# Gate products of the second chunk moved behind the V blocks in a fused gated-delta-rule and spline-FFN kernel

## The reference

```python
q = short_conv(hidden_states @ Wq, conv_wq).reshape(b, t, NUM_HEADS, HEAD_K)
k = short_conv(hidden_states @ Wk, conv_wk).reshape(b, t, NUM_HEADS, HEAD_K)
v = short_conv(hidden_states @ Wv, conv_wv).reshape(b, t, NUM_HEADS, HEAD_V)
beta = jax.nn.sigmoid(hidden_states @ Wb)
g = -jnp.exp(A_log) * jax.nn.softplus(hidden_states @ Wa + dt_bias)
o = gated_delta_rule(q, k, v, g, beta)
gate = (hidden_states @ Wg).reshape(b, t, NUM_HEADS, HEAD_V)
o = o * jax.lax.rsqrt(jnp.mean(o * o, -1, keepdims=True) + EPS) * norm_weight
o = o * jax.nn.silu(gate)
return o.reshape(b, t, VALUE_DIM) @ Wo
```

## Time and profile before

| what | us |
|---|---|
| median of 3 runs | 807.68 |
| the three runs | 807.45, 812.63, 807.68 |
| the profiled execution | 812.1 |
| its span, first to last instruction | 810.3 |

### The profile page before, as it was taken

The page is one execution under the profiler, slowest core; times in us unless marked ns, Lnnn a source line. Parts: engine busy times, 40 slices in busy tenths (PEclk is TensorE's granted clock), DMA queues, the critical chain, the costliest instruction groups (busy, mean ns, idle before and its releaser), DMA issues.

```text
span 810.3 us, 15480 instructions
## 1 busy us (share of the span) xinstructions
PE 759.3 (94%) x5688; PEld 448.3 (55%) x5688; DVE 580.9 (72%) x1403; ACT 468.6 (58%) x1082; POOL 357.5 (44%) x393
## 2 busy tenths in 40 slices
PE   2979599999999999999899999999899999999998
PEld 1456267656657665656674656755344444444443
DVE  5789957878998979998978998577764544545320
ACT  3777835675795766796765687666643333333310
POOL 5148966675894653784663678123330000000000
PEclk9999958999999999999999999999999999999999
DMA  7420041140003022003022001168954414304111
GB/s 216 140 91 18 0 111 40 51 149 12 31 5 124 23 93 79 27 0 126 14 104 80 27 1 34 62 197 179 207 177 104 118 39 104 92 14 111 45 37 42
DMA packets 56113, 63.26 MB, mean 78 GB/s; under 512 B 18375, under 2 KB 41276, under 8 KB 56038
## 3 DMA queue, kind: packets, MB, share of 16 engines
q1 hardware_dynamic: 49430, 45.50, 20.0%
q0 software_dynamic: 4224, 13.11, 5.6%
q10 hardware_dynamic: 2384, 3.67, 1.3%
HBM read 33.69 MB, written 19.73 MB: 66 GB/s over the span
## 4 chain that ended last, share of the span: by engine, by line
PE 70%; DVE 20%; issue 4%; ACT 4%; POOL 1%; DMA 1%; DVEq 0%; POOLq 0%; ACTq 0%
PE bank L672 22%; PE pd L2121 7%; PE pd L2120 7%; PE pd L2119 7%; DVE bank L1213 3%; DVE inv L1219 3%; PE bank L768 2%; DVE cv L1115 2%; PE bank L916 2%; PE bank L861 2%; PE bank L839 2%; PE bank L892 2%; PE bank L759 2%; PE pu L2101 2%; PE pu L2102 2%
## 5 line engine op out<-in xcount | busy, mean ns | idle before, releaser
L672 PE MATMUL bank<-x_parts,w 128*128 128x512 f16 x576 | 137.0, 385 | 1.8 <-DVE x_parts L1072 1.5
L2188 DVE TENSOR_TENSOR hh<-sg,pu 128x512 f32<-128x512 f32 x64 | 43.9, 687 | 96.1 <-ACT sg L2158 91.2
L672 PEld LDWEIGHTS bank<-x_parts,w 128*128 128x128 f16 x576 | 59.4, 106 | 63.8 <-issue 6.8
L2066 POOL DMA_DIRECT2D yr<-y_attn x16 | 8.8, 552 | 181.8 <-DMA out<-yr 181.8
L672 PE MATMUL bank<-w,x_parts 128*128 128x384 f16 x384 | 80.9, 343 | 6.6 <-DVE inv L1219 6.6
L2158 ACT ACTIVATE sg<-pg 128x512 f32<-128x512 f32 x64 | 38.0, 595 | 71.0 <-PE pg L2102 71.0
L1115 DVE SCALAR_TENSOR_TENSOR cv<-raw,taps,cv 128x512 f32<-128x512 f32 x72 | 56.1, 829 | 0.6
L672 PEld LDWEIGHTS bank<-w,x_parts 128*128 128x128 f16 x384 | 37.0, 110 | 26.3 <-DVE inv L1219 7.4
L1739 POOL TENSOR_TENSOR rn<-t,mhalf 128x6 f32<-128x6 f32 x16 | 22.8, 1422 | 65.2 <-DVE t L1305 65.2
L1213 DVE TENSOR_TENSOR bank<-bank,inv 128x60 f32<-128x60 f32 (+32 forms) x184 | 47.1, 285 | 2.2
L2119 PE MATMUL pd<-dw,it 128*128 128x512 f16 x128 | 48.5, 379 | 0.0
(11 more groups left out here) (302 smaller groups left out, 2064.2 us busy)
## 6 DMA issues: line engine op xcount, KB each, us to landing
xr<-in_x SPq DMA_DIRECT2D x16, 256.0 KB, 2.6
y_attn<-xr SPq DMA_DIRECT2D x16, 256.0 KB
down_rows<-inv SPq DMA_DIRECT2D x8, 512.0 KB, 4.3
yr<-y_attn POOLq DMA_DIRECT2D x16, 256.0 KB, 3.0
out<-yr SPq DMA_DIRECT2D x16, 256.0 KB, 3.1
xb<-in_x SPq DMA_DIRECT2D x3, 1024.0 KB, 5.6
xn_hi<-x_parts POOLq DMA_DIRECT2D x4, 512.0 KB
xn_lo<-x_parts POOLq DMA_DIRECT2D x4, 512.0 KB
```

The lines of the kernel that those rows point to most:

```text
L672: ins = nc.tensor.matmul(out, a, b, start=first and i == 0, stop=last and i == 2)
L2188: v.tensor_tensor(hh[:, i % 2, :], sg[:, i % 2, :], pu[i % 2][:], ALU.mult).then_inc(h_ready, 1)
```

## The change

In every turn the two halves of chunk 1's gate products go behind V5 on PE, and their silus go behind the taps of V5 and the silu of V4 on ACT. The table of banks is changed to the same order. No operation is added or removed.

```diff
@@ -170,8 +170,7 @@
     ring += [("blk", n) for n in range(NQK)] + gates[:2] + [("ktr", c) for c in range(NCH)]
-    for n in range(NV):
-        ring += [("blk", NQK + n)] + (gates[n:n + 1] if n in (2, 3) else [])
+    ring += [("blk", NQK + n) for n in range(NV)] + gates[2:4]
     ring += [("vtr", 0), ("vtr", 1), ("vtr", 2), gates[6], ("vtr", 3), ("vtr", 4), gates[7], ("vtr", 5)]
@@ -967,8 +966,8 @@
                     else:
                         block_products(s, NQK + n)
-                    if n in (2, 3):
-                        gate_products(s, 1, n - 2)
+                for h in range(2):
+                    gate_products(s, 1, h)
                 v_transposes(s, 0)
@@ -1606,8 +1605,8 @@
                     if n >= 1:
                         silu(s, NQK + n - 1)
-                    if n in (1, 2):
-                        gates(s, 1, n - 1)
+                for h in range(2):
+                    gates(s, 1, h)
                 v_tokens(s, 0)
```

## The result

| | before | after |
|---|---|---|
| median of the runs, us | 808.70 (4 runs, 807.45 to 812.63) | 832.84 (4 runs, 829.18 to 834.57) |
| the profiled execution, us | 812.1 | 829.18 |
| its span, us | 810.3 | 827.3 |

After takes 1.0282 times as long, 95% interval 1.025 to 1.0314. Over the 44 runs of before that were taken beside the experiments, the 16 with a mean granted clock of 0.977 to 0.981 have a median of 812.54 us and the other 28 (0.985 and more) one of 808.63; the profiled execution of before, at 812.1 us and 0.981, is like the 16.

A forecast was written before the change was run, and what follows sets the result against it. PE, busy 94% of the span, was taken to bound the kernel. 812.1 + 19.5 (late transposes after give-back) + 3.4 (clock) - 4.2 (first turn) = 830.8 us, range 821 to 841.

The forecast's parts named there:

- The late transposes: Turns two to four: transposes of V0 start 7.6 us late; after give-back 6.5 a turn, 19.5 us in all.
- the base with the first turn: Profiled execution of before, 812.1 us, less 4.2 us expected from the first turn.
- What is given back: Turns two to four: later waits of PE vanish, 0.35 and 0.63 us in the third turn, leaving 6.6 of 7.6.
- partly made up: Rival: other engines get ahead, recurrent parts run 2 to 4 us a turn shorter; 818.4 us, chance 14%.
- The clock behind it: After the 3.4 us wait before V0's transposes, PE's clock falls: 1.7 us in two of three turns, 3.4 us.
- The first turn: Wait for the inversion is cut in two, clock holds in the stretch behind it: -4.2 us, bounds 0 and -10.2.
- the reading of the median: Median run, 807.68 us, read as runs whose first turn was not held back by the clock; 830.6 us on that base.
- 4.2 of 10.2 us: First turn: PE 10.2 us earlier at full clock, but GpSimd's cubics let `rn` start only 4.2 us earlier.
- VectorE covers nothing: Rival at the head of `solve`: a late inversion would hide PE's wait; price 0, 807.9 us, chance 6% with similar outcomes.
- the clock stay low through `solve`: Rival, turns two to four: small products at half rate lose 10.2 us a turn; 858.0, one turn 837.6; chance 10%.

The follow-up runs named there:

- The two experiments on banks and silus: Changed kernel with gate A and gate B in banks outside the ring: 813.76 us; changed kernel with both gate silus ahead of the silu of V4: 817.72 us.
- both together: Changed kernel with gate A in bank 3, gate B in bank 2, and both gate silus ahead of the silu of V4: 809.89 us, 0.9994 of before.
- the kernel whose first turn is as before: Kernel before with the change made in turns two to four only: 828.23 us, 1.0232 of before.

## Why the prediction was right, and where it was not

Forecast 830.8 us, measured 832.84 and 831.78: right in size, and right in the mechanism of turns two to four. That the sum comes so near is in part luck. The late transposes were put 2.8 us too high (19.5 against 16.7, below), and the base with the first turn 2.4 too low (812.1 - 4.2 = 807.9 against the median of 808.70 and 1.6 for the first turn); these errors nearly cancel.

- *The late transposes.* Forecast 7.6 us a turn, measured 7.55, and in the same steps: waits of 1.1, 1.1, 2.1 and 3.4 us were forecast, 0.94, 0.88, 1.78 and 3.26 measured. The starts match more closely than the waits: V5, gate A, gate B and the transposes were forecast 15.7, 19.4, 23.4 and 28.7 us after V0 and stand 15.71, 19.36, 23.26 and 28.65 after it; the idle time of a row is counted from a modelled end. The two experiments on banks and silus show both causes; neither remedy is enough alone, both together take the loss away.
- *What is given back.* Forecast 1.0 to 1.1 a turn, measured 7.55 - 5.42 = 2.1 in the third turn. Between the transposes and the state products it was 1.2, about as forecast. The rest was missing in the working: PE's wait of 1.23 us for the state, which shrank to 0.34. In the second turn it is 7.55 - (6.60 - 1.69) = 2.6, where 1.69 is the clock's part. In the fourth it is 1.2; there before had no such wait. The term is 4.91 + 5.42 + 6.32 = 16.7 us and not 19.5. This much of the rival "partly made up" was true.
- *The clock behind it.* Forecast 1.7 us in two of three turns, 3.4. Three profiles with the changed order in turns two to four hold nine such waits; six were followed by a fall, which cost 11.2 us together, 3.7 per execution. In the profile of after it was only one of three. The Trainium skill (TensorE: Matmul & The Clock Gate, "Why this matters for your kernels") would have every gap paid for; here three of nine waits of the same length were not.
- *The first turn.* Forecast -4.2 us by the change. This step failed. The profile of after does look like it: the wait for the inversion is cut in two, the gate products of chunk 2 start before it is over, and the stretch behind it runs at clock 1.00.

```profile
97.40 1.09 PE L775 MATMUL bank<-ident,vT 128*128 128x128 f32 x8 [3.26 <-ACT gate L1468]
98.33 2.11 PE L671 MATMUL bank<-w,x_parts 128*128 128x384 f16 x12
101.00 2.12 PE L671 MATMUL bank<-w,x_parts 128*128 128x384 f16 x12 [0.56 <-DVE inv L1218]
...
138.00 1.54 PE L925 MATMUL bank<-ident,BA 128*128 128x128 f32 x6 [5.03 <-DVE BA L1311]
```

But this comes without the change too. V0 of turn 2 is 210.02 - 207.06 = 2.96 us earlier in after than in before, and 210.02 - 206.50 = 3.52 us earlier in the kernel whose first turn is as before; 0.25 and 0.60 of these stood already at V0 of the first turn, ahead of anything that was moved. And the kernel with both gate silus early, whose PE has the changed order, has the long stretch at the low clock (columns as above):

```profile
101.00:127.00 26.00, 26.00 (x379) 0.55 0.30 83
```

So the long stretch at 0.50 belonged to the profiled execution, as the reading of the median had it, and should have been no term of the change. Only one execution of before was traced: that its runs with the higher mean clock lack the stretch is read from their clocks and times. Whether the change makes the stretch rarer stays open; none of the 12 runs with the change in the first turn alone has so low a mean clock, but the execution just shown has.

GpSimd then sets the pace, as forecast: `rn` starts at 134.92 in after (135.4 forecast), and VectorE's input to L925 waits for it.

```profile
134.92 1.33 POOL L1738 TENSOR_TENSOR rn<-t,mhalf 128x6 f32<-128x6 f32 x1
```

The wait of 5.03 us before L925 is what the prediction left unnamed when it counted 4.2 of 10.2 us; the clock of 0.57 behind it (136 to 144) was not forecast. Neither comes from the change: the kernel whose first turn is as before has 3.43 us and 0.57 there. What the change does bring in the first turn is a fall of the clock behind the 3.26 us, in two of three profiles: in the kernel with the change there alone and in the changed kernel run again. In the first of these the clock is 0.50 until 104 us, and the 24 gate products of chunk 2 take 6.00 us instead of 4.06 (third turn of after, above):

```profile
98.64 1.97 PE L787 MATMUL bank<-ident,vT 128*128 128x128 f32 x8 [3.26 <-ACT gate L1482]
100.41 6.00 PE L683 MATMUL bank<-w,x_parts 128*128 128x384 f16 x24
```

From V0 of the first turn to V0 of the second it is 139.75 and 140.18 us in these two profiles, 138.84 in after, without the fall, and 138.63 in the kernel whose first turn is as before. That points to the fall as the cause of the first turn's 1.6 us (interval 0.1 to 3.9), but it was not tried apart; executions also differ by up to 2.5 us before V0 of the first turn, with code that no kernel changed.

- *The sum, by what was measured:* 16.7 + 3.7 + 1.6 = 22.0 us; the two sets of runs gave 24.1 and 21.4.
- *The rivals.* VectorE covers nothing in turns two to four (no wait for the inversion there), and in no profile did the clock stay low through `solve` in these turns.

## What to carry to other kernels

Where two products alternate between PSUM banks, an instruction can wait not for its input but for whoever reads the use of the bank before it (here 3.26 us a turn, for a silu); on moving work, ask who that reader becomes, what stands ahead of it in its own queue, and what is queued behind the waiting instruction. The cure is then a bank of its own or an earlier reader, and here it took both. When one profiled execution is the base of a sum, a stretch that only some executions show, such as a low clock, is no term of the change: compare the profile's time with the median first, and keep the two apart.

## What the runs showed of the hardware that was not expected

After the same wait of 3.24 to 3.26 us in front of the same work, PE's granted clock fell to 0.50 in six of nine cases and stayed at 1.00 in three; what decides stays open. A fall cost 1.7 us in five cases and 2.8 in one. In the first turn the granted clock behind the wait for the inversion was 0.50 for 27 us in the profile of before and 0.91 on average in that of a kernel with the same first turn: one order of instructions has two clocks. The two executions are 3.5 us apart at V0 of turn 2, 2.9 of them since V0 of the first turn (141.55 us against 138.63).
